# A graph and expert network on one core: pad rows ahead of the sorted tokens, roots of the third normalization on ScalarE and VectorE, scatters alone on GpSimd

## What is computed

```
x = x + graph_attention(layernorm(x), adj)          # masked softmax over neighbours
x = x + thirty_steps(layernorm(x))                  # tanh, silu, layernorm, linear; 30 times
x = x + relu(h @ Wa + (adj @ h) @ Wb + bias)        # h = layernorm(x)
x = x + moe(layernorm(x))                           # below

def moe(t):                                         # t: 16384 tokens
    logits = t @ Wr + br                            # 8 experts
    top_p, top_idx = top_k(softmax(logits), 2)
    w = top_p / sum(top_p)
    xn = layernorm(t)
    y_e = gelu((xn * g_e + b_e) @ W1_e + b1_e) @ W2_e + b2_e
    return sum over the two chosen e of w_e * y_e
```

## Time and profile before

| | us |
|---|---|
| median of three runs | 2563.8 |
| the profiled execution | 2566.49 |
| its span | 2564.7 |
| TensorE busy | 2378.7 (93%) |
| VectorE busy | 2081.9 (81%) |
| GpSimd busy | 2027.5 (79%) |
| ScalarE busy | 1811.9 (71%) |
| TensorE's mean granted clock | 0.969 of full |

### The profile page before, as it was taken

The page is one execution under the profiler, slowest core; times in us unless marked ns, Lnnn a source line. Parts: engine busy times, 40 slices in busy tenths (PEclk is TensorE's granted clock), DMA queues, the critical chain, the costliest instruction groups (busy, mean ns, idle before and its releaser), DMA issues.

```text
span 2564.7 us, 60894 instructions
## 1 busy us (share of the span) xinstructions
PE 2378.7 (93%) x19678; PEld 2320.6 (90%) x19935; DVE 2081.9 (81%) x5761; ACT 1811.9 (71%) x2185; POOL 2027.5 (79%) x1592
## 2 busy tenths in 40 slices
PE   6829999999999999999999999999862999999998
PEld 5829999999999999999999999989861999999998
DVE  5999999999999999999999999987572444444443
ACT  3779999999999999999999999833210334344333
POOL 4769999999999999999999999995764444444443
PEclk9969999999999999999999999999885999999999
DMA  9100000000000000000000000003223555555554
GB/s 261 69 1 1 0 0 0 0 0 0 0 0 0 0 0 0 0 0 0 0 0 0 0 0 0 0 18 110 75 73 109 212 216 212 211 214 216 212 212 148
DMA packets 121574, 164.56 MB, mean 64 GB/s; under 512 B 14982, under 2 KB 74018, under 8 KB 121360
## 3 DMA queue, kind: packets, MB, share of 16 engines
q1 hardware_dynamic: 111792, 145.12, 16.6%
q0 software_dynamic: 9088, 17.14, 2.0%
q10 hardware_dynamic: 608, 1.30, 0.2%
HBM read 40.40 MB, written 24.65 MB: 25 GB/s over the span
## 4 chain that ended last, share of the span: by engine, by line
DVE 58%; PE 31%; issue 7%; POOL 1%; DMA 1%; ACT 1%; SPq 1%; another core or an unknown queue 0%; DVEq 0%; POOLq 0%; ACTq 0%
DVE pair_stats L661 25%; DVE state L704 18%; PE psum L1265 11%; PE psum L1256 11%; DVE state L683 6%; PE psum L1094 5%; PE psum L1084 2%; DVE it_vars L665 2%; DVE x_stats L661 1%; POOL sorted_rows L556 1%; DVE resid L731 1%; PE psum L1213 1%; DMA sorted_rows<-state,slot 1%; PE psum L1246 1%; DVE state L700 1%
## 5 line engine op out<-in xcount | busy, mean ns | idle before, releaser
L1094 PEld LDWEIGHTS psum<-w_ffn,turned 128*128 128x128 f32 x7680 | 1010.1, 192 | 36.0
L1094 PE MATMUL psum<-w_ffn,turned 128*128 128x128 f32 x7680 | 1013.7, 275 | 12.8 <-issue 0.2
L512 POOL TENSOR_TENSOR it_rstd<-it_vars,minus_half 128x8 f32<-128x8 f32 x480 | 785.5, 1636 | 0.0
L515 POOL TENSOR_TENSOR state<-state,it_rstd 128x768 f32<-128x768 f32 x480 | 708.0, 1475 | 37.6
L661 DVE BATCH_NORM_STATS2 pair_stats<-state 128x6 f32<-128x256 f32 x1920 | 685.1, 418 | 0.0
L1084 PE MATMUL psum<-ident,state 128*128 128x128 f32 x4352 | 595.6, 281 | 59.1 <-DVE state L700 42.8
L704 DVE SCALAR_TENSOR_TENSOR state<-state,psum 128x1024 f32<-128x1024 f32 x464 | 560.8, 1209 | 1.8 <-ACT state L964 0.9
L1084 PEld LDWEIGHTS psum<-ident,state 128*128 128x128 f32 x4352 | 479.5, 143 | 78.0 <-issue 57.7
L957 ACT COPY turned<-psum 128x1024 f32<-128x1024 f32 x480 | 485.8, 1012 | 80.4 <-PE psum L1084 43.9
L967 ACT ACTIVATE state<-state 128x1024 f32<-128x1024 f32 x480 | 512.7, 1068 | 28.6 <-DVE state L700 9.1
L964 ACT ACTIVATE state<-psum 128x1024 f32<-128x1024 f32 x464 | 481.0, 1037 | 0.0
(11 more groups left out here) (190 smaller groups left out, 1725.2 us busy)
## 6 DMA issues: line engine op xcount, KB each, us to landing
adjT<-resid SPq DMA_DIRECT2D x312, 320.0 KB
adjT<-sorted_rows SPq DMA_DIRECT2D x156, 66.5 KB, 1.8
resid<-in_x_dram SPq DMA_DIRECT2D x16, 512.0 KB, 7.3
state<-in_adj_dram SPq DMA_DIRECT2D x16, 512.0 KB, 7.3
adjT_dram<-adjT SPq DMA_DIRECT2D x7, 512.0 KB, 3.7
adjT<-adjT_dram SPq DMA_DIRECT2D x7, 512.0 KB, 3.5
out_dram<-resid,adjT POOLq DMA_INDIRECT x156, 2.4
sorted_rows<-state,slot POOLq DMA_INDIRECT x128
```

The lines of the kernel that those rows point to most:

```text
L512: nc.gpsimd.tensor_tensor(it_rstd[s % 8][:, :], it_vars[s % 4][:, :], minus_half[:, 0:TILES], ALU.pow).then_inc(it_pow, 1)
L515: nc.gpsimd.tensor_tensor(values[s][:, 0:POOL_TILES, :], values[s][:, 0:POOL_TILES, :], wide(it_rstd[s % 8][:, 0:POOL_TILES]), ALU.mult).t ...
L1094: last = nc.tensor.matmul(dst[:, t, :], stationary(t), moving(t), start=bias is None and m == 0, stop=m == len(terms) - 1, skip_group_chec ...
```

## The change

1. *Region layout.* A region now has its 128 pad rows first and then the tokens (`REGION = SLAB + TOKENS`, `region_0` starts at `SLAB`). All pads are written by two DMAs on SyncE as soon as GpSimd's constants are there (`pair_tables`), ahead of the loads of away-kept masks. The 29 fills, `pad_rows`, `pad_row`, `pad_out` and `ends_ready` are gone.
2. *Last slab of a region.* It ends at the region's last token and may overlap the slab before, or the pads. New tables (`slab_last`, `slab_from`, a fourth column in `slab_has` and `diag`) give `slab_skip`, which GpSimd adds to the token numbers of a slab (`store_at`), so that repeated rows fall out of bounds.
3. *Roots.* The root of the third normalization's variance is taken by ScalarE (`Sqrt` into `row_root`), and VectorE makes its reciprocal and one Newton step at the head of `route`, five linked operations ahead of L796's; `ROUTE_STEPS` is 20, and TensorE waits for step 6 (`LOGITS_READ`).
4. *Scatters.* GpSimd's loop holds only scatters. Each half has its own semaphore, and a half waits until the same half of the stream before has landed, in every stream from the second on.
5. *Scaling for the third layer.* GpSimd scales tiles 0 to 3, ScalarE tiles 4 to 7, as four activations a stream (`scale_inputs`), 3 slots behind, in the tail's slots and the first five of the pipeline. TensorE waits for both.

```diff
-    REGION = TOKENS + SLAB
+    REGION = SLAB + TOKENS
...
+            sp.wait_ge(pair_tables, 1)
+            regions = sorted_rows[0:PAIRS * REGION, :].rearrange("(c r) w -> r c w", c=PAIRS)
+            no_token = pad[:, :].bitcast(F32)
+            sp.dma_start(regions[0:SLAB], no_token.unsqueeze(1).to_broadcast([P, PAIRS, ROW])).then_inc(pads_in, 16)
+            sp.dma_start(sorted_rows[PAIRS * REGION:PAIRS * REGION + SLAB, :], no_token).then_inc(pads_in, 16)
...
-            sp.wait_ge(pad_out, 16)
-            sp.wait_ge(ends_ready, 1)
-            for c in range(SP_FILLS):
-                fill(sp, c)
...
-            sp.wait_ge(pads_in, 16 * (PAIRS + 1))
-            sp.wait_ge(scattered, 16 * STREAMS * TILES)
+            sp.wait_ge(pads_in, 16 * 2)
+            for h in range(2):
+                sp.wait_ge(scattered[h], 16 * STREAMS * TILES // 2)
...
             for s in range(STREAMS):
+                if s >= 4:
+                    pool.wait_ge(x2_scaled_a, s - 3)
                 pool.wait_ge(x2_var_ready, s + 1)
                 rsqrt(x_rstd[s % 4][:, :], x_var[s % 4][:, :], x2_pow, s)
-                nc.gpsimd.tensor_tensor(values[s], resid[s], wide(x_rstd[s % 4][:, :]), ALU.mult
-                                        ).then_inc(x2_scaled, 1)
                 nc.gpsimd.tensor_copy(state[s][:, :, TOKEN].bitcast(I32), ids[:, s * TILES:(s + 1) * TILES])
+                nc.gpsimd.tensor_tensor(values[s][:, 0:X2_POOL, :], resid[s][:, 0:X2_POOL, :],
+                                        wide(x_rstd[s % 4][:, 0:X2_POOL]), ALU.mult).then_inc(x2_scaled, 1)
...
-                    ).then_inc(scattered, 16)
...
+                    ).then_inc(scattered[2 * t // TILES], 16)
+
+            for m in range(STREAMS):
+                pool.wait_ge(columns_ready, m + 1)
+                pool.wait_ge(slots_ready, m + 1)
+                for h in range(2):
+
+                    if m > 0:
+                        pool.wait_ge(scattered[h], 16 * TILES // 2 * m)
+                    scatter(m, range(TILES // 2 * h, TILES // 2 * (h + 1)))
...
+                nc.gpsimd.tensor_tensor(store_at[n % EACH][:, :], rows_in[n % EACH][:, TOKEN:TOKEN + 1].bitcast(I32),
+                                        slab_skip[:, n:n + 1], ALU.add).then_inc(store_known, 1)
...
-                dve.wait_ge(x3_pow, s + 1)
+                guess, w = row_guess[s % 2][:, 0, :], row_guess[s % 2][:, 1, :]
+                dve.wait_ge(x3_root, s + 1)
+
+                linked(nc.vector.reciprocal(guess, row_root[s % 4][:, :]))
+                linked(nc.vector.tensor_tensor(w, guess, guess, ALU.mult))
+                linked(nc.vector.tensor_tensor(w, w, row_vars[s % 4][:, :], ALU.mult))
+                linked(nc.vector.tensor_scalar(w, w, -0.5, 1.5, ALU.mult, ALU.add))
+                linked(nc.vector.tensor_tensor(row_rstd[s % 4][:, :], guess, w, ALU.mult))
...
+            def scale_inputs(s):
+                act.wait_ge(x2_pow, s + 1)
+                for t in range(X2_POOL, TILES):
+                    last = nc.scalar.activation(values[s][:, t, :], resid[s][:, t, :], ACT.Copy,
+                                                scale=x_rstd[s % 4][:, t:t + 1])
+                last.then_inc(x2_scaled_a, 1)
+
+            for k in range(EVAC_LAG):
+                iteration(STEPS, tail=True, slots=range(k, k + 1))
+                if k >= X2_LAG:
+                    scale_inputs(k - X2_LAG)
...
+                if k < STREAMS - EVAC_LAG + X2_LAG:
+                    scale_inputs(k + EVAC_LAG - X2_LAG)
...
-            for c in range(SP_FILLS, PAIRS + 1):
-                fill(act, c)
+                if r is not None:
+                    act.wait_ge(x3_var_ready, r + 1)
+                    if r >= 4:
+                        act.wait_ge(route_step, ROUTE_STEPS * (r - 4) + 1)
+                    nc.scalar.activation(row_root[r % 4][:, :], row_vars[r % 4][:, :], ACT.Sqrt).then_inc(x3_root, 1)
```

More of the change, by code:

```diff
@@ L90, in network @@
         psW = psum[:, 7, :]
-        psT = [psum[:, j, 0:3 * P].rearrange("p (v j) -> p v j", v=3) for j in range(2)]
+        psT = [psum[:, j, :].rearrange("p (v j) -> p v j", v=4) for j in range(2)]
         resid_all = sb("resid", [P, STREAMS, TILES, D])
@@ L112, in network @@
         row_rstd = [sb(f"row_rstd{j}", [P, TILES]) for j in range(4)]
+        row_root = [sb(f"row_root{j}", [P, TILES]) for j in range(4)]
+        row_guess = [sb(f"row_guess{j}", [P, 2, TILES]) for j in range(2)]
         soft = [sb(f"soft{j}", [P, 3, TILES]) for j in range(2)]
@@ L143, in network @@
         pair_end = sb("pair_end", [P, PAIRS])
-        pad_row = sb("pad_row", [P, PAIRS], I32)
         slab_ends = [sb(f"slab_ends{j}", [P, PAIRS]) for j in range(2)]
         past = sb("past", [P, 2, PAIRS])
-        past_steps = sb("past_steps", [P, 2, 4, PAIRS])
-        slab_is = sb("slab_is", [P, 2, 4])
-        slab_has = sb("slab_has", [P, 2, 3])
+        past_steps = sb("past_steps", [P, 2, 5, PAIRS])
+        slab_is = sb("slab_is", [P, 2, 5])
+        slab_has = sb("slab_has", [P, 2, 4])
+        slab_from = sb("slab_from", [P, 2])
+        slab_last = sb("slab_last", [P, 2])
         slab_row = sb("slab_row", [P, 2 * P], I32)
         slab_exp = sb("slab_exp", [P, 2 * P, 2], I32)
+        slab_skip = sb("slab_skip", [P, 2 * P], I32)
+        store_at = [sb(f"store_at{j}", [P, 1], I32) for j in range(EACH)]
         pad = sb("pad", [P, ROW], I32)
@@ L266, in network @@
         x2_scaled = sem("x2_scaled")
+        x2_scaled_a = sem("x2_scaled_a")
         x2_flip = sem("x2_flip")
@@ L288, in network @@
         slots_ready = sem("slots_ready")
-        scattered = sem("scattered")
+        scattered = [sem(f"scattered{h}") for h in range(2)]
         fold_ready = sem("fold_ready")
@@ L317, in network @@
         out_rows = out.rearrange("b n d -> (b n) d")
-        ROUTE_STEPS, PLACE_STEPS = 15, 6
+        ROUTE_STEPS, LOGITS_READ, PLACE_STEPS = 20, 6, 6
         prep_ready = [0]
+        table_at = [0]
         block = ctx.enter_context(nc.Block())
@@ L372, in stages @@
                     yield base + j, j % STREAMS
-        def by_queue(rows):
-            return rows.rearrange("r c -> (r c)").rearrange("(q n) -> q n", q=16)
-        def fill(queue, c):
-            if c < PAIRS:
-                at = queue.value_load(pad_row[0:1, c:c + 1], min_val=c * REGION, max_val=c * REGION + TOKENS)
-                dst = sorted_rows[bass.ds(at, SLAB), :]
-            else:
-                dst = sorted_rows[PAIRS * REGION:PAIRS * REGION + SLAB, :]
-            queue.dma_start(by_queue(dst), by_queue(pad_rows)).then_inc(pads_in, 16)
-        SP_FILLS = 10
         @block.sync
@@ L594, in store @@
             def store(n):
+                pool.wait_ge(store_known, n + 1)
                 pool.wait_ge(y_ready, n + 1)
@@ L873, in _ @@
             steps = pair_steps[:, 1, :]
-            nc.vector.tensor_copy(pad_row[:, :], pair_end[:, :]).then_inc(ends_ready, 1)
+            nc.vector.tensor_scalar(part_of[:, :], slab_j[:, 0:1], 1.0 / P, None, ALU.mult)
+            nc.vector.tensor_tensor(pair_steps[:, 4, 0:PAIRS - 1], pair_end[:, 1:PAIRS], pair_end[:, 0:PAIRS - 1],
+                                    ALU.subtract)
             table(nc.vector.tensor_tensor(steps, pair_end[:, :], region_0[:, :], ALU.subtract))
@@ L901, in _ @@
             for h in range(2):
-                last = nc.vector.tensor_tensor(diag[:, h], ident[:, :].unsqueeze(1).to_broadcast([P, 3, P]),
-                                               slab_has[:, h, :].unsqueeze(2).to_broadcast([P, 3, P]), ALU.mult)
-            last.then_inc(diag_ready, 1)
+                last = nc.vector.tensor_tensor(diag[:, h], ident[:, :].unsqueeze(1).to_broadcast([P, 4, P]),
+                                               slab_has[:, h, :].unsqueeze(2).to_broadcast([P, 4, P]), ALU.mult)
+            table(last)
             dve.wait_ge(table_psum, 1)
@@ L1008, in _ @@
                 iteration(q)
-            iteration(STEPS, tail=True, slots=range(EVAC_LAG))
+            def scale_inputs(s):
[8 more added lines that the diff above has]
+                    scale_inputs(k - X2_LAG)
             for k in range(GNN1_SLOTS):
```

66 lines of the change are left out of this document (23 added, 43 removed).

## The result

The kernel after took 2584.26 us (2582.27 to 2585.62, 4 runs), the kernel before 2562.96 us (2561.05 to 2568.02, 4 runs): ratio 1.0079, interval 1.0064 to 1.0093. It is slower, where I had forecast 2550.7 and faster. The profiled execution took 2585.08 us, span 2583.2.

The account below looks back on a forecast made before the run. The last scatter was taken to release the experts. 16.5 us of landing waits less 2.7 later start, 0.3 overhead and 0.3 expert start gave 13.2, taken as 13.1: 2550.7 us from the 2563.8 median, range 2541 to 2561.

Parts of the forecast that it names:

- (b): TensorE's six slots after slot 7: VectorE's added Newton work makes them 2 us later, between nothing and 4.2.
- (c): Slots 14 to 17, where VectorE also folds expert weights: 0.5 us later, bounds 0 to 2.
- Rival B: Slots 8 to 13: scatters without roots between lengthen TensorE's issue waits; 53% more cancels the gain, 80% gives 2570; chance 0.11.
- Waits for landings: Last four streams' 32 scatters: waits for earlier scatters to land vanish, 16.5 us less; bounds all or half.
- per-burst overhead: A 0.3 us cost subtracted in the final sum, named there only as extra.
- Root off GpSimd: GpSimd's scatter loop: a stream falls from 11.7 to 10.1 us, but worth nothing at the end.
- main term: Scatter waits in the last four streams: 16.5 us less, as each half waits only for the previous stream's same half.
- (a): Newton on VectorE, five linked operations, 1.05 us a stream; VectorE becomes longer than TensorE, so slot 7 pays 0.7 us.
- (d): Slot 18: logits wait for VectorE's L796, now behind the five new operations, the full 1.05 us later.
- The tail: End of the second stage, scaling shared with ScalarE: first mix product 0.3 us earlier, bounds 2 earlier to 1 later.
- Table switches: ScalarE alternating Exp and Sqrt: two loads a slot, 2.6 us, hidden at cost 0; bounds 0 to 8.
- Pads, tables, experts: Pads land before 1690 at cost 0; tables and weights ready at 1959.6, before rows at 1961.4; expert start costs 0.3 us.

Follow-up runs that it names:

- stalling: Sittings where the kernel before took 2562.6 to 2563.5 us; the unchanged kernel after took 2584.3 and 2583.8, ratios 1.0079 and 1.0083.
- calm: Sittings where the kernel before took 2551.6 to 2552.2 us; the unchanged kernel after took 2534.9, ratio 0.9932.
- the counters alone: Kernel before with only two counters of landed scatters, one per half, so a half waits for the previous stream's same half: 2568.2 us, ratio 1.0021.

## Why the prediction was wrong, by its own steps

| us, after less before | forecast | stalling | calm |
|---|---|---|---|
| cast for stream 12 | +3.95 | +32.0 | +8.5 |
| first of the last 32 scatters | +2.7 | +31.6 | -4.9 |
| the last 32 scatters | -16.5 | -13.1 | -14.1 |
| first row load | -13.4 | +19.0 | -18.5 |

*The step that failed* is (b), slots 8 to 13, and with it (c). I had seen that these slots are long, by 24.7 us in six, and took that for a fact of the stage: the 2 us of (b) are for the Newton step alone, and the sum has nothing for a change in the stalls. Rival B had it, and I put it low because "their number is the same, and a root is only 1.6 us in 11.7". The trace of before held the answer: its issue waits stand beside rows of 8 scatters and beside none of 4. I had read one line of them and the pitch of the scatters, and never laid the one over the other. The root was not 14% of GpSimd's time but what cut the rows. (The 24.7 us are also not "waits on issue in all", as B has it, but the excess length of the slots; of issue waits there are 10.4.)

Between the first cast and stream 12's the kernel before took 1914.76 - 1753.63 = 161.1 us, after 1946.72 - 1760.58 = 186.1: 25 of the 32 us are here. By the calm profiles the Newton step and the rest of the change cost 4.9 of them (137.8 against 132.9, forecast 4.25), and the stalls, 28.2 us before and 48.3 after, the other 20.1. B bounded them to six slots. In truth they cost the first seven slots 24.7 us before and 30.7 after, and the five up to stream 12's, where before no row of 8 ran, 3.5 and 17.6; for these (c) has 0.5. The other 7 us are at the first cast. 3.0 of them were there when stage two began (its first product at 195.86 against 192.86); between the other profiles of the two kernels that is 1.6 and 1.2, so a part is of the execution and not of the change.

*Waits for landings*: right in kind, 13.1 and 14.1 instead of 16.5. No wait for a landing is left. Of the 3.4 us over 31 gaps of 1.26, in the profile of the result, 1.3 are a wait for stream 13's slots and 1.6 a gap within a half (at 1972.02, released by "issue"), whose cause I do not know. The 0.3 us "per-burst overhead" of my sum stands on no row.

*Root off GpSimd*, which I took for worth nothing: right where there are stalls, wrong in a calm sitting. There the slots of the kernel before come each 9.8 us, GpSimd with 11.8 a stream falls behind, and when stream 12's slots are written at 1886.70 its scatter begins at 1901.08, 14.4 us late, 2.15 of it for a landing. Without the root GpSimd keeps up: 1895.22 and 1896.16. This term alone turns +8.5 into -4.9, and it is why the calm result, 17.3 us by the medians (2552.2 - 2534.9), is above my 13.1. That the two are no farther apart is luck: 13.4 us of this term, which I had at nothing, stand against 3.6 us lost at the first cast, where I had a gain of 0.3, and against 2.4 us less of the main term.

*Newton step* (a, b, d): 0.55 us in each of seven slots in a calm sitting (10.35 against 9.8), where (a) said 0.7 for slot 7, and 1.1 us in the slot before stream 12's cast (14.3 against 13.2), as (d) said. VectorE's slack in "slow" slots, with which I cut (b), exists only with stalls. (c) was nothing: 12.2, 12.2 and 13.7 us in both.

*The tail* (e): forecast 0.3 us earlier, bounds 2 earlier to 1 later. The first `q` copy comes 3.6 us later in calm sittings (1713.69 against 1710.09), and 2.0 of them are the divided scaling, by the run with the scaling on GpSimd (1711.72); 1.2 were there when stage two began. In the tail ScalarE stood 8.05 us for GpSimd's root of stream 0, and TensorE 4.95 us for the copy (L959) that ScalarE makes behind its four tiles; TensorE's clock then fell to 0.50 (its 1.2 GHz level, 1680 to 1684.5), and eight matmuls took 1.91 us instead of 1.05:

```profile
1678.16 1.28 ACT L1014 ACTIVATE state<-resid,x_rstd 128x128 f32<-128x128 f32 x4 [8.05 <-POOL x_rstd L484]
1680.39 0.61 PE L1104 MATMUL psum<-bias_mv,ones_bf 128*128 128x512 bf16 x1 [4.95 <-ACT turned L959]
1680.79 1.91 PE L1108 MATMUL psum<-w_ffn,turned 128*128 128x128 f32 x8
```

The pace of 2.85 us a stream was right (1678.35 and 1681.20). The term that I left out is the order on ScalarE: its four tiles wait there for the root, and the copy that TensorE needs stands behind them.

*Table switches*: right. In each slot two loads, each 1.28 us, and the one for `Exp` runs ahead of its wait. The kernel after, calm:

```profile
1780.33 1.28 ACT L1051 ACT_TABLE_LOAD   x1
1781.62 0.21 ACT L1051 ACTIVATE row_root<-row_vars 128x8 f32<-128x8 f32 x1
1781.85 1.28 ACT L1028 ACT_TABLE_LOAD   x1
1786.58 0.22 ACT L1028 ACTIVATE parts<-parts 128x16 f32<-128x16 f32 x1 [3.45 <-DVE parts L815]
```

From the end of the first load to the instruction behind it there is 0.01 us, so no drain shows. The Trainium skill ("ScalarE: Activation LUTs", section "What ACT_TABLE_LOAD costs") gives 2.66 us for a switch, a load of 1.28 and a drain of 1.38. The load agrees with this trace and the drain does not; the measurement decides.

*Pads, tables, experts*: the pads cost nothing, as said. That the fills lay "on nobody's path" holds for the kernel before, but no longer once the scatters do not wait, by the run with the counters alone. The expert stage was unchanged.

*What stays open.* Shown is that in a stalling sitting the loss follows the rows without a break: 48, 36 and 21 us of stalls with no, short and long breaks. Open is why a sitting stalls; I did nothing that turned one kind into the other. Why TensorE's instructions come late beside rows of scatters is not settled either. The Trainium skill's page "Runtime: NRT & Kernel Launch", section "Instruction fetch mechanics", says that each sequencer fetches its instructions by a DMA queue of its own, in blocks of 16 KiB, mostly hidden. The profile does list such queues (q8, 37 packets, 0.61 MB), so a late block is a candidate. Against it: from 1760 to 1880 there are 7 and 6 packets on the two such queues where it stalls, and 7 and 7 in the calm sitting; the window of the stall at 1783 to 1787 has none; and the issue waits come in many small steps and not in one. No run tested it. The late results after 1900 speak for another candidate: what reaches the other engines late there are the signals of TensorE's matmuls, or their ends, which the profile only models. Not shown either.

## What to carry to other kernels

Before an operation is taken off an engine, ask what its pauses did for others: sort the unexplained waits of the bottleneck by what the neighbouring engine does at that moment, and do not go by their mean. A break of 1.6 us after 4 scatters (2555.1 and 2539.6) is faster than the kernel before in both kinds of sitting, the tighter kernel only in one; a gain of under 1% should be measured in more than one sitting. And test a main term alone: the two counters without the early pads gained 13 us of scatters and lost them to fills that they had exposed.

## What the runs showed of the hardware that I had not expected

- The same program on the same inputs takes 2583.8 us in one sitting and 2534.9 in another, 1.9% apart, where its runs in one sitting lie within 4.1 us; the kernel before differs by 11 us, the one with a long break by 15, the one with short breaks by 36. The longer the unbroken rows, the larger the gap.
- In a stalling sitting a row of 8 indirect scatters (1.26 us each) slows TensorE from about 8 us into it; rows of 4 with 1.64 us of other work or a wait behind them did not; rows of 4 with 0.58 us between them did, about half as much (12.8 us of issue waits against 25.5).
- In a calm sitting 24 scatters in a row cost TensorE nothing measurable: 137.8 us for twelve slots, against 137.6 with no scatter beside them.
